# Feed-forward stage in 4 blocks of 400 tokens instead of 5 of 320, its rounded weights loaded by DMA

## What is computed

```python
x = x + xattn(layernorm(x), ctx_2048, itok, ...)
# feed-forward: 512 -> 1408 -> 512, weights with values -1, 0, 1, scales per output
xf = layernorm(x)
g = einsum('th,ih->ti', xf, gate_w) * gate_s
u = einsum('th,ih->ti', xf, up_w) * up_s
hdn = silu(g) * u
x = x + einsum('ti,hi->th', hdn, down_w) * down_s
```

## Time and profile before

| what | us |
|---|---|
| median of 3 runs (lowest, highest) | 760.04 (757.87, 764.9) |
| the profiled execution | 759.56 |
| its span, first to last instruction | 757.8 |
| attention ends, feed-forward products begin | 536.5 |
| first block's end, then one block | 582.8, then 42.33 each |

### The profile page before, as it was taken

The page is one execution under the profiler, slowest core; times in us unless marked ns, Lnnn a source line. Parts: engine busy times, 40 slices in busy tenths (PEclk is TensorE's granted clock), DMA queues, the critical chain, the costliest instruction groups (busy, mean ns, idle before and its releaser), DMA issues.

```text
span 757.8 us, 17572 instructions
## 1 busy us (share of the span) xinstructions
PE 714.1 (94%) x6970; PEld 664.7 (88%) x6970; DVE 442.1 (58%) x940; ACT 395.7 (52%) x886; POOL 200.2 (26%) x330
## 2 busy tenths in 40 slices
PE   4999898999998999999999999989999999999997
PEld 4888778779987998779987899779899999999996
DVE  2999836754566536755467446767463545536242
ACT  5888744673457535674357535688382323323130
POOL 1656855604063312604054301630000000000000
PEclk9999999999999999999999999999999999999999
DMA  8999754244314433044313442039111212020111
GB/s 282 344 378 314 267 154 98 63 92 89 98 28 109 89 70 88 19 124 88 92 37 111 90 83 72 3 122 373 36 36 36 71 36 69 6 79 18 36 54 35
DMA packets 46363, 81.28 MB, mean 107 GB/s; under 512 B 5482, under 2 KB 30106, under 8 KB 46282
## 3 DMA queue, kind: packets, MB, share of 16 engines
q1 hardware_dynamic: 40796, 53.67, 26.5%
q0 software_dynamic: 5488, 26.50, 10.2%
HBM read 57.26 MB, written 11.28 MB: 90 GB/s over the span
## 4 chain that ended last, share of the span: by engine, by line
PE 73%; DVE 9%; DMA 6%; ACT 5%; issue 3%; SPq 2%; POOL 1%; DVEq 0%; POOLq 0%
PE ps L1461 17%; PE ps L1169 13%; PE ps L1021 11%; PE ps L1499 8%; PE ps L1174 6%; PE ps L1097 4%; DMA kv_table<-tab 4%; PE ps L1070 3%; PE ps L194 3%; ACT q_lat L1207 2%; SPq L921 2%; PE ps L1032 2%; PE ps L1061 2%; PE ps L1086 1%; PE ps L844 1%
## 5 line engine op out<-in xcount | busy, mean ns | idle before, releaser
L1311 DVE TENSOR_TENSOR o_parts<-q_lat,o_parts 128x320 fp32r<-128x320 f32 x80 | 68.2, 870 | 67.6 <-ACT o_parts L1215 67.6
L1169 PE MATMUL ps<-o_parts,wvo_hi 128*128 128x320 f32 x320 | 96.8, 313 | 1.8 <-ACT o_parts L1215 1.8
L1169 PE MATMUL ps<-o_parts,wvo_lo 128*128 128x320 f32 x320 | 95.7, 310 | 0.0
L1215 ACT ACTIVATE o_parts<-q_lat 128x320 fp32r<-128x320 f32 x80 | 63.9, 821 | 45.0 <-PE ps L1169 44.9
L1546 ACT ACTIVATE silu<-ps,ffn_scale 128x320 f32<-128x320 f32 x55 | 29.0, 527 | 97.5 <-PE ps L1461 96.9
L959 POOL TENSOR_TENSOR rot_c<-gathered,cosq 128x192 f32<-128x192 f32 x40 | 25.0, 624 | 162.8 <-PE ps L1032 150.3
L1594 DVE SCALAR_TENSOR_TENSOR hidden<-ps,ffn_scale,silu 128x320 f32<-128x320 f32 x55 | 30.2, 549 | 61.2 <-ACT silu L1546 54.9
L1169 PEld LDWEIGHTS ps<-o_parts,wvo_hi 128*128 128x128 f32 x320 | 60.6, 189 | 2.3 <-ACT o_parts L1215 2.0
L1169 PEld LDWEIGHTS ps<-o_parts,wvo_lo 128*128 128x128 f32 x320 | 60.4, 189 | 0.3
L1174 PE MATMUL ps<-o_parts,wvo_hi 128*128 128x320 f32 x320 | 60.1, 309 | 0.0
L538 PE MATMUL ps<-wkv,ctx_hi 128*128 128x384 f32 x192 | 52.7, 384 | 5.1 <-ACT ctx_hi L402 5.1
(11 more groups left out here) (167 smaller groups left out, 1747.2 us busy)
## 6 DMA issues: line engine op xcount, KB each, us to landing
ctx_raw<-ctxT_dram SPq DMA_DIRECT2D x16, 722.0 KB, 9.1
gathered<-key_rows SPq DMA_DIRECT2D x240, 47.2 KB
head_w<-head_w_dram SPq DMA_DIRECT2D x16, 576.0 KB, 7.8
ffn_raw<-ffn_w_dram POOLq DMA_DIRECT2D x11, 768.0 KB, 12.9
kv_table<-tab POOLq DMA_DIRECT2D x16, 288.0 KB, 6.6
rows<-x_dram SPq DMA_DIRECT2D x5, 640.0 KB, 5.2
residual<-x_dram SPq DMA_DIRECT2D x20, 160.0 KB, 2.3
x_rows<-residual SPq DMA_DIRECT2D x20, 160.0 KB, 2.0
```

The lines of the kernel that those rows point to most:

```text
L1169: last = pe.matmul(ps[:, 4 + m, 0:TB], w[wt][:, h, cols], o_hi[h % RING], start=(h == 0 and n == 0), stop=False, skip_group_check=True)
L1215: act.activation(o_hi[h % RING], q_lat[:, h % 2, :, h // 2], ACT.Copy).then_inc(oh_ok, 1)
L1311: dve.tensor_tensor(o_lo[h % RING], q_lat[:, h % 2, :, h // 2], o_hi[h % RING].bitcast(F32), ALU.subtract).then_inc(ol_ok, 1)
```

## The change

The stage works on FB = 4 blocks of FT = 400 tokens in tiles of FLT = 100 rows. Norm and residual helpers take the tile's size (80 in the attention, 100 in the stage). The first x tiles go to places of their own (`ffn_x_hi`, `ffn_x_lo`, over weights of the attention's queries) and no longer to rowsT and four. The rounded weight parts are no longer made by ACT: POOL loads each chunk a second time, with source and destination as float32r, into a `short` tile. Chunks 0 to 3 of raw and chunk 1 of short are loaded when the last block's query products are done; the other raw chunks and short 0 at the point where all raw loads stood; short 2 to 8 after the last o product; short 9 and 10 after the oT transposes. ACT reduces 6 chunks' low bits and DVE 5 (4 and 7 before). low_parts moves into the attention's part, ahead of DVE's oT copies. PE's oT transposes move ahead of take_flag.

```diff
+FT = 400
+FLT = FT // NLT
+FB = TOK // FT
-FRONT = 7
-EARLY = 3
-ACT_PARTS = (3, 5, 7, 9)
+SOON = 4
+OVER = 208
+ACT_PARTS = (0, 2, 4, 6, 8, 10)
...
+            short[1] = sb("ffn_short1", [P, WR], F32R, plain)
...
+            for c in (2, 3):
+                short[c] = sb(f"ffn_short{c}", [P, WR], F32R, places)
+                width += WR
             sb("ffn_gap", [P, 2 * H * D - width], F32, places)
+            xT_hi, xT_lo = (sb(f"ffn_x_{part}", [P, KC, FT], F32R, places) for part in ("hi", "lo"))
             ffn["raw"] = sb("ffn_raw", [P, IC, WR], F32, places)
-            ffn["hi_front"] = sb("hi_front", [P, FRONT, WR], F32R, places)
+            sb("ffn_space", [P, OVER], F32, places)
+            short[0] = sb("ffn_short0", [P, WR], F32R, places)
+            for c in range(4, IC):
+                short[c] = sb(f"ffn_short{c}", [P, WR], F32R, places)
...
+        def load_weights(c):
+            pool.dma_start(ffn["raw"][:, c, :], a["ffn_w"][c]).then_inc(ffn_in[c], 16)
+
+        def load_short(c):
+            pool.dma_start(ffn["short"][c][:, :], a["ffn_w"][c].bitcast(F32R)).then_inc(short_in[c] if c < 2 else ffn_in[c], 16)
...
+            if last:
+                pool.wait_ge(q_mm, c24(b, len(q_out)))
+                for c in range(SOON):
+                    load_weights(c)
+                load_short(1)
...
         pool.wait_ge(av_mm, BLOCKS * STEPS)
-        for c in range(IC):
-            pool.dma_start(ffn["raw"][:, c, :], a["ffn_w"][c]).then_inc(ffn_in[c], 16)
+        for c in range(SOON, IC):
+            load_weights(c)
+        load_short(0)
+        pool.wait_ge(o_mm, c16(BLOCKS - 1, H))
+        for c in range(2, 9):
+            load_short(c)
+        pool.wait_ge(bt_mm, NLT * BLOCKS)
+        for c in range(9, IC):
+            load_short(c)
...
-                if last and h % 3 == 0:
-                    sum_halves(act, ACT_PARTS[(h - 6) // 3])
-                if last and h % 3 == 2 and h >= 8:
-                    split_high(act, (h - 8) // 3)
+                if last and h % 2 == 0:
+                    sum_halves(act, ACT_PARTS[(h - RING) // 2])
...
             if last:
-                for c in DVE_PARTS[(H - RING) // 2:]:
-                    join_bits(dve, c, bits_dve)
+                low_parts()
             dve.wait_ge(o_mm, c16(b, H))
...
                 if first:
-                    pe.wait_ge(whi_ok, c + 1)
+                    if c < 2:
+                        pe.wait_ge(short_in[c], 16)
+                    else:
+                        pe.wait_ge(ffn_in[c], 32)
...
-                    return pe.matmul(ps[:, 2 * which + c % 2, 0:TB], wt(part, c, which, k), xs, skip_group_check=True,
+                    return pe.matmul(ps[:, 2 * which + c % 2, 0:FT], wt(part, c, which, k), xs, skip_group_check=True,
                                      **flags)
...
                 if first and c == 0:
+                    attn_turn_back(pe, BLOCKS - 1)
                     some_low = take_flag()
                 with pe.If(some_low != 0):
                     exact()
...
-                if first and c == 0:
-                    attn_turn_back(pe, BLOCKS - 1)
...
-                if first and c + EARLY < IC:
-                    split_high(act, c + EARLY)
```

More of the change, by code:

```diff
@@ L114, in build @@
         ident = sb("ident", [P, P])
-        rows = sb("rows", [LT, NLT, D])
+        rows = sb("rows", [FLT, NLT, D])
+        short = {}
+        with ExitStack() as plain:
+            short[1] = sb("ffn_short1", [P, WR], F32R, plain)
         with ExitStack() as plain:
@@ L122, in build @@
             four32 = sb("four32", [P, KC, TB], F32, plain)
-        rowsT = sb("rowsT", [P, KC, TB], F32R)
+        sb("rowsT_place", [P, KC, TB], F32)
         four = sb("four", [P, KC, TB], F32R)
-        ln_q = NormStage("lnq", sb, sem, rows, rowsT32, None, ps, ident)
-        ln_f = NormStage("lnf", sb, sem, rows, rowsT, four, ps, ident)
-        sums = [sb(f"residual{i}", [LT, D]) for i in range(2)]
+        ln_q, ln_f = (NormStage(tag, sb, sem, rows, size, ps, ident) for tag, size in (("lnq", LT), ("lnf", FLT)))
+        ln_q.into(rowsT32, None)
+        sums = [sb(f"residual{i}", [FLT, D]) for i in range(2)]
         scale = sb("ffn_scale", [P, 2 * IC + KC])
@@ L161, in build @@
                 shared = build_attention(nc, block, ctx, a, w, ffn, ps, ident, table, x1, rows, rowsT32, four, low_mass,
-                                         ln_q, ln_f, sums, qc, fetch, setup)
-                build_ffn(nc, block, ctx, a, ffn, ps, ident, x1, rows, rowsT, four, ln_f, sums, scale, shared,
-                          low_mass, low_any, low_flag)
+                                         low_any, ln_q, ln_f, sums, qc, fetch, setup)
+                build_ffn(nc, block, ctx, a, ffn, ps, ident, x1, rows, xT_hi, xT_lo, ln_f, sums, scale, shared,
+                          low_any, low_flag)
 class Fetch:
@@ L679, in unrolled, with __init__ @@
         body(b, b == 0, b == BLOCKS - 1)
-def ffn_high(ffn, c):
-    return ffn["hi_front"][:, c, :] if c < FRONT else ffn["hi_back"][:, c - FRONT, :]
 class Residual:
-    def __init__(self, tag, sem, rows, src, dst):
-        self.src, self.dst, self.rows = src, dst, rows
+    def __init__(self, tag, sem, rows, size, src, dst):
+        self.src, self.dst, self.size, self.rows = src, dst, size, [r[0:size, :] for r in rows]
         self.loaded = [sem(f"{tag}_in{i}") for i in range(2)]
@@ L730, in finish, with build_attention @@
             sp.wait_ge(s, 32 * BLOCKS)
-def build_attention(nc, block, ctx, a, w, ffn, ps, ident, table, x1, rows, rowsT, four, low_mass, ln, ln_f,
+def build_attention(nc, block, ctx, a, w, ffn, ps, ident, table, x1, rows, rowsT, four, low_mass, low_any, ln, ln_f,
                     sums, qc, fetch, setup):
@@ L1312, in low_latent, with low_parts @@
                               ALU.subtract).then_inc(ol_ok, 1)
+        def low_parts():
+            dve.wait_ge(bits_act, len(ACT_PARTS))
+            dve.wait_ge(bits_dve, len(DVE_PARTS))
+            dve.tensor_scalar(low_mass[:, :], low_mass[:, :], 0.0, None, ALU.not_equal).then_inc(any_step, 1)
+            dve.wait_ge(any_step, 1)
+            dve.tensor_reduce(low_any[:, :], low_mass[:, :], AX.X, ALU.max).then_inc(any_step, 1)
         adds, stats = (5, 7, 13, 17), (3, 9, 15, 21)
@@ L1363, in _, with build_ffn @@
         unrolled(dve, body)
-    return (res, turn_back, add_back, ffn_x_in, split_high, whi_ok, bits_act, bits_dve)
-def build_ffn(nc, block, ctx, a, ffn, ps, ident, x1, rows, rowsT, four, ln, sums, scale, attention,
-              low_mass, low_any, low_flag):
+    return (res, turn_back, add_back, ffn_x_in, short_in, ffn_in, any_step)
+def build_ffn(nc, block, ctx, a, ffn, ps, ident, x1, rows, xT_hi, xT_lo, ln, sums, scale, attention,
+              low_any, low_flag):
     def sem(name):
@@ L1378, in build_ffn @@
     h_hi, h_lo, act_g, hf, oT = (ffn[s] for s in ("h_hi", "h_lo", "silu", "hidden", "yT"))
-    xT_hi, xT_lo = rowsT, four
-    attn_res, attn_turn_back, attn_add_back, x_in, split_high, whi_ok, bits_act, bits_dve = attention
+    attn_res, attn_turn_back, attn_add_back, x_in, short_in, ffn_in, any_step = attention
     s_in, tail_in, tail_out = sem("scale_in"), sem("tail_in"), sem("tail_out")
-    any_step, any_mm, flag_ok = (sem(s) for s in ("any_step", "any_mm", "flag_ok"))
-    res = Residual("fres", sem, sums, x1, a["out"])
+    any_mm, flag_ok = sem("any_mm"), sem("flag_ok")
+    res = Residual("fres", sem, sums, FLT, x1, a["out"])
     g_mm, u_mm, silu_ok, hf_ok, hh_ok, hl_ok, d_mm, d_act, d_dve, y_mm = (
@@ L1422, in _ @@
     def _(pool):
-        with pool.Fori(1, BLOCKS) as b:
+        with pool.Fori(1, FB) as b:
             ln.root(pool, b)
@@ L1428, in wt @@
         cols = slice(which * KC * P + k * P, which * KC * P + (k + 1) * P)
-        return ffn_high(ffn, c)[:, cols] if part == "hi" else ffn["raw"][:, c, cols]
+        return ffn["short"][c][:, cols] if part == "hi" else ffn["raw"][:, c, cols]
     @block.tensor
@@ L1530, in _ @@
         some_low = body(0, True, False, None)
-        with pe.Fori(1, BLOCKS - 1) as b:
+        with pe.Fori(1, FB - 1) as b:
             body(b, False, False, some_low)
-        body(BLOCKS - 1, False, True, some_low)
+        body(FB - 1, False, True, some_low)
     @block.scalar
@@ L1621, in body @@
                     dve.wait_ge(y_mm, c4(b, t + 1))
-                    dve.tensor_tensor(rows[:, t, :], ps[0:LT, 6 + t % 2, :], rows[:, t, :],
+                    dve.tensor_tensor(rows[:, t, :], ps[0:FLT, 6 + t % 2, :], rows[:, t, :],
                                       ALU.add).then_inc(res.summed, 1)
         dve.wait_ge(s_in, 16)
-        low_parts()
         low_flag_out()
         body(0, True, False)
-        with dve.Fori(1, BLOCKS - 1) as b:
+        with dve.Fori(1, FB - 1) as b:
             body(b, False, False)
-        body(BLOCKS - 1, False, True)
+        body(FB - 1, False, True)
 def constants():
```

109 lines of the change are left out of this document (52 added, 57 removed).

## The result

The change made the kernel slower: 770.6 us as the median of 4 runs (766.05 to 776.06) against 759.76 us of 4 runs of the kernel before, a ratio of 1.0128 (95% interval 1.0077 to 1.018). The forecast was 753.3 us, with a range up to 761. The profiled execution took 766.05 us, its span is 764.3 us.

A forecast was written before the change was run, and what follows sets the result against it. PE, busy 94% of 757.8 us, was taken as the bound. Terms of -3.4 - 2.4 + 0.3 - 3.2 + 1.9 = -6.8 us gave 752.8 from 759.56, or 753.3 on the median's footing; range 749.5 to 761.

The forecast's parts named there:

- Term 1: Feed-forward products: 1320 of 320 columns become 1056 of 400 at 180 ns, a gain of 3.4 us.
- Term 2: One feed-forward block fewer saves y transposes and a seam, together -2.4 us; longer x copies in attention cost +0.3.
- Term 3: Entry of the feed-forward stage: earlier low_parts and transposes cut extra time from 3.8 to 0.6 us, a gain of 3.2.
- Term 4: Eleven added weight loads land near the raw 2.03 us each; PE waits only from 3.1 us, so no cost.
- rivals b: Converting weight loads at half the rate, 4.1 us each: PE waits 8.9 us in block 0, 762 us; chance 0.13.
- Rival (c): Converting loads at 6.3 us each: PE waits 28.7 us at chunks 2 to 10 of block 0, 782; chance 0.10.
- term 5: Four closing stores: tiles of 100 rows use 10 engines, +1.8 us, and +0.1 for the longer yT copy.
- rival (d): Closing stores of 100 rows take 16 engines: 1.5 us less, 751.8 us; chance 0.10.
- (a): Stage entry keeps its cost, the clock still falls: gain 1.0 instead of 3.2, 755.5 us; chance 0.10.

The follow-up runs named there:

- e3: Kernel before with only the changed stage entry (low_parts ahead of oT copies, oT transposes ahead of the flag's read): 760.75 us, 0.9976.
- e6: Kernel before with the changed stage entry and the residual adds of attention tiles 2 and 3 after chunk 7: 758.67 us, 0.9961.
- e1: Changed kernel with VectorE's residual adds of attention tiles 2 and 3 moved from chunk 1 to after chunk 7 of the first block: 754.0 us, 0.9907.
- e7: Changed kernel with POOL waiting for residual tiles 2 and 3 to land before issuing short loads of chunks 4 to 8: 763.77 us, 1.002.
- e10: Unedited repeat of the changed kernel with the residual adds of tiles 2 and 3 after chunk 7: 755.2 us, 0.9904.
- e4: Changed kernel with residual adds after chunk 7 and the last four stores split into 80 and 20 rows: 751.25 us, 0.9884.
- e2: Changed kernel without short loads of chunks 2 to 10, whose products use rounded weights of chunks 0 and 1: 754.75 us, 0.9926.

## Why the prediction was wrong

*Term 1, the products*: the mechanism was right, the size not. 182.2 ns against the 180 taken and the bound of 184: 1056 x 0.1822 = 192.4 us, a gain of 1.1 instead of 3.4. Each product has 15.5 ns beyond its 400 columns, not 13.3. So what a product costs beyond its columns grew a little with them. The Trainium skill ("TensorE: Matmul & The Clock Gate", Back-to-back issue gap) gives the formula that the prediction quotes against itself, n / 2.4 + 2.5 ns, for an isolated product and not for a stream of weight loads and products. An estimate by it for 400 columns is 169.2 ns; this stream measured 182.2.

*Term 2, transposes and seams*: right, and the seams a little better (some 0.5 us each, 0.8 before). Five blocks of 42.33 against four of 51.72 are 4.8 us, where terms 1 and 2 said 5.8.

*Term 3, the entry*: right. 7.85 us became 5.0 for products that take 0.6 longer, a gain of 3.4 with no fall of the clock (3.2 forecast). What the step left out is what the slow entry covered: it didn't ask what is late next when PE reaches chunk 1 some 3 us sooner. e3 and e6 show it: the residual.

*Term 4, the weights*: this is the step that failed. It asked when the short loads would be late for PE, by an unknown rate, and they weren't: the rate, 2.3 us per load, is near the raw 2.03, under the 3.1 from which PE would wait, and rivals b and c fall with it. Rival (c) said of it "DMA moves little else then" and named the residual's transfers only as something that might slow the loads. The other direction decided: the loads slowed the residual's stores from 2.0 to 6.1 and 8.1 us, its loads from 2.2 to 7.5 and 8.1. That VectorE's program has these adds behind chunk 1, ahead of the next `hidden`, stood in the kernel; term 5 named such a wait, for residual tiles "after chunk 3", where the middle blocks have them, and not for the first block, where they are after chunk 1. The hole on PE is 10.8 us, and the half clock behind it cost 1.7 more (109 products in 21.55 us instead of 19.9). The first block took 64.55 us by the chain of waits instead of e1's 52.06: 12.5 us, of the 12.6 that lie between the forecast for the stage and the result.

*Term 5, the tail*: right. From the last product (755.60) to the end 8.7 us against 7.2 before (757.8 - 750.61), +1.5 where 1.9 was forecast, 10 engines per store as forecast; rival (d) falls. The working counted 14 slices before, where the earlier trace rows have 15 with traffic. By the Trainium skill ("DMA: Bandwidth & Descriptors", Why a DMA increments its semaphore by 16 and not by 1) a transfer takes the largest number of engines up to 16 that divides the slowest dimension of both sides, 10 for 100 partitions. The trace agrees: 40 small packets of 4 stores.

*The other rivals*: (a) didn't happen, the clock was granted in full until the hole. (c) was right in its sign and its place, the first block, and in nothing else: its price was on PE's wait for loads, which e7 alone shows.

With the one wait out of the way (e1 and e10, 0.9907 and 0.9904), the sum of the terms stands: -6.8 us forecast, and 214.1 against 221.3 us for the stage alone, -7.2, beside the -7.1 of the terms that lie in it. That this is so close is in part luck: term 1 gave 2.3 us too little, and the seams, the entry and the tail together 1.9 more than forecast. Both are faster than the kernel before and than the changed one; e4 is the same with the split stores.

## What to carry to other kernels

When loads are added to a stretch, price them in both directions: when they come, and what every other transfer there then takes; here a small transfer on another queue took three to four times as long beside a full one. For each of those find who waits for it and what is queued behind that wait on its engine: an add that could come 17 us later without loss (e1) cost 11 because it stood ahead of the operation that PE needed. And when a slow place is made fast, list what it was covering.

## What wasn't expected of the hardware

Loads with a float32r source and destination, 768 KB each, land nearly as quickly as plain ones from the same queue: 12.2 us median against 12.9 before, and nine in a row 2.3 us apart on average (1.9 at the closest) with four transfers of the residual between them, against 2.0.

Two stores of 160 KB on SP's queue took 6.1 and 8.1 us beside nine queued loads of POOL's, 5.8 and 5.9 beside four, and 2.0 and 2.2 beside none (e2). How the engines share between the queues, these runs don't settle.

After the hole of 11 us ten products of 400 columns ran at 333 ns each, exactly 400 columns at the lower level of 1.2 GHz, before the full clock came back.
